# A recommender's attention kernel on one core: where a superblock's scores stand between projection, keys and spread on TensorE

## The reference, cut to what matters

```python
cand = candidate_features @ Wi + bi                      # 128 -> 64
hist = history_features @ Wi + bi                        # (512, 200, 64)
hidden = relu((cand @ Wq)[:, None, :] + hist @ Wk)
scores = where(mask, hidden @ Wv, -1e9)                  # (512, 200)
attn = softmax(scores, axis=1)
interest = einsum('bs,bse->be', attn, hist)
avg = sum(hist * mask, axis=1) / history_length
x = concatenate([interest, cand, avg])                   # then three small layers with
                                                         # batch norm and ReLU, and a sigmoid
```

## Time and profile before

| what | value |
|---|---|
| median of 3 runs | 221.59 us (221.26 to 221.71) |
| the profiled execution: its own time, and its span | 222.31 us, 220.2 us |
| busy: PE, DVE, ACT, POOL | 206.5, 174.7, 103.7, 62.5 us |
| PE weight loads (PEld) | 81.1 us |
| HBM read | 53.32 MB, 242 GB/s over the span |

### The profile page before, as it was taken

How to read it: one execution, slowest core, us unless ns; L and a number is a source line. 1 busy time by engine, 2 the same in 40 slices (tenths; PEclk the granted TensorE clock), 3 DMA queues, 4 the chain that set the end, 5 groups by cost and what they waited for, 6 DMA issues and landing times.

```text
span 220.2 us, 6280 instructions
## 1 busy us (share of the span) xinstructions
PE 206.5 (94%) x2110; PEld 81.1 (37%) x2110; DVE 174.7 (79%) x1087; ACT 103.7 (47%) x302; POOL 62.5 (28%) x112
## 2 busy tenths in 40 slices
PE   6899999999999999999999999999999998976593
PEld 2432333334343433333434343343434433423321
DVE  0327665897979797979797998979797979798970
ACT  2025545355546363645555453555463635552423
POOL 8903014060606050413224150606060503322000
PEclk9999999999999999999999999999999999999955
DMA  5999999696969797887969696969697870000000
GB/s 172 374 422 419 419 308 323 253 315 225 336 216 328 255 307 277 277 319 265 320 222 326 231 324 255 315 227 338 208 343 244 290 293 4 0 3 0 4 0 0
DMA packets 10225, 53.72 MB, mean 244 GB/s; under 512 B 1105, under 2 KB 2001, under 8 KB 10194
## 3 DMA queue, kind: packets, MB, share of 16 engines
q1 hardware_dynamic: 10194, 53.32, 69.3%
HBM read 53.32 MB, written 0.00 MB: 242 GB/s over the span
## 4 chain that ended last, share of the span: by engine, by line
PE 87%; DVE 5%; DMA 2%; issue 2%; ACT 2%; SPq 1%; DVEq 0%; ACTq 0%
PE hist_ps L388 43%; PE key_ps L401 24%; PE score_ps L412 10%; PE attn_ps L430 5%; DVE scratch L533 3%; DMA history<-history_dram 2%; DVE kept L520 1%; PE score_ps L462 1%; PE score_ps L457 1%; PE score_ps L454 1%; ACT x L320 1%; ACT hidden L300 0%; PE attn_ps L370 0%; PE key_ps L443 0%; PE hist_ps L430 0%
## 5 line engine op out<-in xcount | busy, mean ns | idle before, releaser
L300 ACT ACTIVATE hidden<-key_ps,query 128x200 f32<-128x200 f32 x256 | 88.6, 429 | 92.9 <-PE key_ps L401 92.9
L388 PE MATMUL hist_ps<-history,params 128*64 128x400 f32 x512 | 103.0, 523 | 2.5 <-DMA history<-history_dram 1.6
L520 DVE SCALAR_TENSOR_TENSOR kept<-item,lens,hist_ps 128x200 f32<-128x200 f32 x256 | 93.8, 418 | 13.9 <-PE hist_ps L388 13.9
L533 DVE CUSTOM_DVE_ANT_0 scratch<-attn_ps,kept 128x200 f32<-128x200 f32 x236 | 72.1, 362 | 17.6 <-PE attn_ps L430 17.6
L401 PE MATMUL key_ps<-kept,params 64*64 64x400 f32 x512 | 58.2, 523 | 2.2 <-ACT hidden L300 1.4
L388 PEld LDWEIGHTS hist_ps<-history,params 128*64 128x64 f32 x512 | 30.9, 138 | 43.7 <-issue 26.4
L254 POOL TENSOR_SCALAR attn<-weights,inv_sum 128x200 f32<-128x200 f32 x15 | 6.5, 435 | 122.2 <-DVE inv_sum L548 122.2
L401 PEld LDWEIGHTS key_ps<-kept,params 64*64 64x64 f32 x512 | 13.8, 132 | 42.6 <-issue 34.5
L412 PE MATMUL score_ps<-hidden,wv_rows 128*32 128x200 f32 x512 | 25.1, 336 | 0.0
L430 PE MATMUL attn_ps<-parts,spread 64*64 64x200 bf16 x472 | 21.2, 250 | 2.6 <-DVE parts L620 2.2
L430 PEld LDWEIGHTS attn_ps<-parts,spread 64*64 64x64 bf16 x472 | 13.3, 106 | 24.4 <-issue 15.9
(11 more groups left out here) (67 smaller groups left out, 57.8 us busy)
## 6 DMA issues: line engine op xcount, KB each, us to landing
history<-history_dram SPq DMA_DIRECT2D x63, 800.0 KB, 5.0
history<-history_dram SPq DMA_DIRECT2D x2, 400.0 KB, 4.9
candT<-candidates_dram SPq DMA_DIRECT2D x1, 256.0 KB, 5.4
params<-parameters_dram SPq DMA_DIRECT2D x1, 248.5 KB, 12.2
params<-parameters_dram SPq DMA_DIRECT2D x1, 226.5 KB, 2.5
lens_raw<-lengths_dram SPq DMA_DIRECT2D x1, 136.0 KB, 4.1
probability<-result SPq DMA_DIRECT2D x1, 2.0 KB
```

The source lines that it names most:

```text
L300: act.activation(hidden[:, g % HID_SLOTS, v, :], key_ps[:, v, at * SEQ:(at + 1) * SEQ], ACT.Relu, bias=query[:, 2 * g + v:2 * g + v + 1]). ...
L388: product = pe.matmul(hist_ps[64 * h:64 * h + 64, g % 2, 0:QCOLS], param("wi"), history[:, slot, h, 2 * at:2 * at + 2, :].rearrange("f p s ...
L520: dve.scalar_tensor_tensor(out=kept[:, g % KEPT_SLOTS, u, :], in0=item[:, :], scalar=pair_len[:, col:col + 1], in1=hist_ps[:, g % 2, u * S ...
L533: dve.tensor_tensor_reduce(scratch[:, at, v, :], banks[:, at, v * SEQ:(v + 1) * SEQ], kept[:, q % KEPT_SLOTS, v, :], 1.0, 0.0, ALU.mult, A ...
```

## The change: what it does

In each score iteration `score(j)` is issued before `keys(unit - 1)` and no longer behind it:

```diff
@@ -474,14 +474,14 @@
                 project(2 * unit + 1)
                 if unit == 0:
                     queries()
-                if unit >= 1:
-                    keys(unit - 1)
                 j, at = divmod(unit - SCORE_AT, SB_UNITS)
                 if at == 0 and j >= 0:
                     if j == 0:
                         pe.wait_ge(wv_ready, 1)
                         pe.wait_ge(cand_ready, 1)
                     score(j)
+                if unit >= 1:
+                    keys(unit - 1)
                 if unit >= DELAY:
                     if unit == DELAY:
                         pe.wait_ge(spread_made, 1)
```

## The result

| | before | changed |
|---|---|---|
| median, first set of 6 executions each | 221.43 us (221.16 to 222.05) | 218.65 us (217.48 to 219.70) |
| ratio | | 0.987 (0.984 to 0.990) |
| profiled execution: its time, and its span | 222.31, 220.2 us | 218.46, 216.3 us |

The changed kernel is faster, by 2.8 us where 1.55 were forecast, and its time lies under the forecast range (219.2 to 220.9). Two later sets of the same pair gave less: 220.23 for 221.54 us, ratio 0.992 (0.989 to 0.996), and 220.43 for 221.47 us. Over everything that was run of the two kernels, 30 and 69 executions, the means are 219.68 and 221.36 us: 1.7 us. The first set lies under the forecast range, the two later ones (220.23 and 220.43) inside it. So two questions stand: whether the loop did what the prediction said, and what makes one set give 2.8 us and another 1.0.

What follows compares the result with a forecast made beforehand. TensorE's pace between stages bounds the loop; a superblock is 7.86 us set by VectorE plus 3.82 by TensorE. 13 x 0.12 = 1.56, with 0.03 off and 0.02 added, gives 1.55 us: 221.59 to 220.0 us, range 219.2 to 220.9.

Steps and rivals of the forecast that it cites:

- The steps of a score iteration: TensorE in the loop: projection to scores 1.50, scores to keys 1.49, keys to spread 0.72; 3.71 us in place of 3.82.
- Rival A: Switch from projection to scores, both 128 rows, costs nothing (1.39 us): 1.04 us more won, 219.0 us; chance 0.08.
- The cover: VectorE's idle before the spread stays, 1.06 us of 1.18; the loop of keys and ReLUs costs 0.01 us at most.
- rival C: Loop of keys and ReLUs becomes the bound behind each score iteration: slower, 227.3 or 222.8 us; chance 0.06.
- rival B: Nothing won at keys to spread, weights not loaded early, or VectorE keeps the difference: 221.6 us; chance 0.09.
- The superblock's saving: Each of 13 superblocks, spread to spread, falls from 11.68 to 11.56 us: 0.12 each, 1.56 us.
- The first score iteration: Before any spread covers the ReLUs: 0.16 us lost, 0.13 won back in the second score iteration, 0.03 lost in all.
- The end of the kernel behind it runs off the same semaphores and moves as it is: Behind the last score iteration's spread: the ending only moves earlier, with 0.02 us for the shorter step.
- a few tenths either way: In the ending: a start 1.5 us earlier may move TensorE work between full and half granted clock.

Runs made afterwards that it cites:

- e8: Changed kernel with 21 dummy matmuls in the ending's gaps, first score iteration in its old order (keys, then scores): 218.53 us, ratio 0.985.
- e6: Changed kernel with 21 dummy matmuls in the ending's gaps, the keys' wait for the masked sums left out except in the last unit: 218.09 us, ratio 0.984.
- the fillers: 21 dummy matmuls in TensorE's four gaps behind the loop, added to the kernel before (219.49 us) and to the changed kernel (217.72 us).
- e3: Kernel before with 21 dummy matmuls in the four gaps of TensorE behind the loop: 219.49 us, ratio 0.989.

## Why the prediction was right and wrong

- **The steps of a score iteration: right.** 1.50, 1.49, 0.72 and 0.28 us, each to 0.01. Projection to scores, both of 128 rows, took 1.50 and not 1.39, with the weights at the matmul's own start. What the Trainium skill says in "TensorEngine Tiling (Array Packing)", section Tiling Modes, that changing the tiling mode drains the engine, fits these two numbers; it gives no price, and no row shows the draining itself. Rival A's mechanism did not happen, though the first set's time (218.65) came near its price (219.0): that nearness is chance.
- **The cover: right.** VectorE idles 1.04 us for 1.06 forecast; the keys behind scores cost nothing (2.50, rival C). Nothing was kept by VectorE (rival B).
- **The superblock's saving was sized small.** I took 0.12 us thirteen times, 1.56 in all. Eleven superblocks gave 0.13: the one read as 11.68 is the shortest of before, most are 11.69, and VectorE's start behind the spread gave the whole 0.02 that I halved. The last two are not like the one that I read: in them the change saved 0.20 and 0.11. Over the loop that makes 1.74 instead of 1.56.
- **The first score iteration: right in kind.** 0.16 us are lost (e8). But 0.09 come back at the second scores, since a matmul with one wait starts earlier than one with two (e6). And the time won in e8 by the old order is gone again by the end of the loop. Net gain 0.06 instead of a loss of 0.03.
- **The step that failed: "The end of the kernel behind it runs off the same semaphores and moves as it is".** In order it does; in time it does not. Its length depends on where the granted clock falls and rises among stages with gaps, and it measured 27.3, 29.0 and 29.3 us in three executions of one kernel, where 28.5 less 0.02 was forecast. I had it as "a few tenths either way". The forecast also took the start of the kernel as it was in one profile, 38.80 us to the first counted spread with 0.03 added; it measured 37.88, 37.63 and 38.03. In the profiled execution of the first set the ending gave 1.24 us and the start 0.92 beside the loop's 1.74; for the set's five others only totals are on record. So the 2.8 us of this set are the loop's gain and luck: the three sets gave 2.8, 1.3 and 1.0 us. The three executions shown beforehand lay within 0.45 us, and I took that for the spread of the measurement; 69 executions of the same kernel reach from 217.25 to 223.46. The range had to be wider, by about 1 us on both sides as an estimate from these sets. The Trainium skill says in "TensorE: Matmul & The Clock Gate", Part 1, of the clock's rise at the start of a kernel, that its place varies from run to run of the same kernel; in these endings the fall and the next rise do so too.
- **Open:** why three profiled executions of the kernel before have endings within 0.02 us, all with the clock full until 209 to 210 us, and three of the changed kernel do not. The start of the ending against the clock's changes could favour one or the other; the fillers show that the clock is the cause, not what places its fall. Open too is what draws out the keys in the twelfth superblock, about 0.07 of the 1.74 us.

## What to carry to other kernels

Put stages of the same tile shape next to each other on TensorE, and count the changes of shape: one fewer made the same keys 0.11 us shorter here, and a timeline read from start to start shows it. What the other three changes cost is not shown, since no run leaves them out. Then ask which engine sets each piece of the period; here moving the scores behind the spread, which changes no count, won another 0.06 to 0.07 us per superblock, because the projection behind the spread no longer came late. And before a gain under 1% is judged by totals, cut the executions at events that all have: the loop's 1.75 us repeated to 0.04, while the totals of three sets gave 2.8, 1.3 and 1.0.

## What the runs showed of the hardware that was not expected

- Keys that wait for one semaphore started 0.05 us behind the last ReLU, with two 0.14 to 0.15 us (2.40 and 2.49 us from keys to keys, e6 and changed). The wait left out in e6 was for a value that the same engine had already waited for, and it still cost 0.09 us.
- Twenty-one dummy matmuls in gaps of 0.7 to 2.2 us kept the granted clock at its full level to the layers and made the kernel 2.0 us faster (e3: 219.49 for 221.54).
